# A four-layer graph network: fourth layer in another order of groups, with each tile's end between the groups

## The chip, the cores and the metric

The kernel runs on one core of a Trainium2 chip. The metric is the device time of one execution in microseconds (us).

## What is computed

`x` holds 4096 nodes of 128 features, `adj` is a sparse 4096 x 4096 matrix whose first nodes have far more neighbours than the last. Each of four layers adds to `x` a function of `h = relu(layernorm(x))` and `adj`. The fourth is an attention over neighbours with four heads of 32 features:

```python
q, k, v = (x @ W + b).reshape(n, H, C)           # for each of the three
attn = jnp.einsum('nhc,mhc->hnm', q, k) / np.float32(np.sqrt(C))
neg = jnp.where(mask[None], -jnp.inf, attn)      # mask = adj == 0
m = jnp.max(neg, axis=-1, keepdims=True)
e = jnp.where(mask[None], 0.0, jnp.exp(neg - m))
alpha = e / jnp.sum(e, axis=-1, keepdims=True)
out = jnp.einsum('hnm,mhc->hnc', alpha, v)       # then to (n, 128)
x_r = x @ Ws + bs
beta = sigmoid(concatenate([out, x_r, out - x_r], axis=-1) @ Wb)
return beta * x_r + (1.0 - beta) * out
```

## The kernel before, in words

The nodes are cut into 32 tiles of 128. While the first layer streams `adj`, lists of each tile's neighbours are made, cut into groups (called quads in the code) of up to 384 neighbours and the tile's own 128. The number of groups depends on the data: every tile has at least one, and some of the first have more. `bounds` holds each tile's first group, `quad_tile` each group's tile, and the groups stand in the order of the tiles.

The fourth layer works group by group. For a group, GpSimd (`gather_nodes(3)`, L797) gathers three blocks of 128 rows of keys and values from the table `kv_table` by indirect DMA. SyncE (`load_adj(3)`) loads the group's mask (L583), its tile's queries (L584) and the tile's own key and value rows (L600). TensorE turns the key rows (`turn_rows`, L1912), makes the four heads' scores (`scores`, L1922), turns the exponentials chunk by chunk (`turn_exps`, L1931), and multiplies them with the values (`values`, L1941). ScalarE takes the exponentials (`exps3`, L1029) and copies keys and even chunks out of the matrix engine's memory. VectorE subtracts the mask and takes the maximum (`scores`, L1575), keeps the running maximum of a tile (`maxima3`, L1583 to L1585; the table `cap` resets it where a new tile begins), copies the odd chunks (`turned3`, L1591) and adds the group's result to its tile's row of `acc3`, scaled by the change of the maximum (`add_up3`, L1603 to L1608).

These are a software pipeline: in step g VectorE copies chunk 3 of g, makes the maxima of g + 2, copies chunk 1 of g + 1 and adds up g (`step3`). SyncE and GpSimd load for g + 3. Each engine has its own queue and waits on semaphores. A step's instructions are written out for 7 turns of 4 steps (`PLAIN = 7`), and the rest is a loop of `further` turns of 4, which is 3 here: 40 steps. In written-out steps the gathers take their indices from `node_flat`; in looped ones from `stage`, into which SyncE loads three columns per group first.

Behind the last step comes `finish3` on VectorE: for each of four tile groups (`FT = 8` tiles, 1024 columns) it divides by the sums (L1627, after one reciprocal L1656), multiplies with gate weights (L1631), sums them (L1634, L1635), subtracts the skip term (L1636), makes the gate of the tile group before (L1640, L1641), and adds to `x_sb` (L1646, `blend`; L1652, `blend_tiles` for the last, eight instructions). ScalarE takes exponentials of the gates and multiplies the tiles by their gates (L1065, L1070, `scale`). SyncE then stores the 512 KB of each tile group (L690).

The second layer runs over the same groups. The third layer multiplies the denser part of `adj` as a dense product on TensorE (`dense`, L1877) and the rest group by group; VectorE copies indices (L1486) and adds each group (L1489) there.

## Time and profile before

| | |
|---|---|
| median of 3 runs | 1197.55 us (1195.87 to 1203.04) |
| the profiled execution | 1189.68 us, of which the span is 1188.0 us |
| TensorE busy | 895.1 us (75%) |
| VectorE busy | 822.4 us (69%) |
| ScalarE busy | 687.1 us (58%) |
| GpSimd busy | 509.9 us (43%) |
| mean granted TensorE clock | 0.85 of 2.4 GHz |

The profile shows one execution. Busy is the time in which an engine works on an instruction; waits and register work are not in it. The span goes from the first to the last instruction. In the rows below DVE is VectorE, ACT ScalarE, PE TensorE (PEld its weight loads), POOL GpSimd, SPq the queue of SyncE. A row of the order of time gives start and length in us, engine, line, operation, what is written and read, and in brackets the idle time of the engine before it and what ended it.

### The profile page before, as it was taken

The numbers are of one execution on the slowest core, as the hardware profiler recorded it, in microseconds if no ns is written. First come the engines' busy times: TensorE is split into PE (matmuls) and PEld (weight loads), VectorE is DVE, ScalarE is ACT, GpSimd is POOL, SyncE is SP. The second block draws the span as 40 slices with busy tenths as digits, with TensorE's granted clock in tenths as the row PEclk, the third lists the DMA queues.
The fourth block names the chain that finished last, engine by engine and source line by source line (L and its number), as shares of the span: only waits on it lengthen the run. The fifth ranks groups of instructions, "written<-read, shape, count | busy, mean of one in ns | idle before, by whom it ended". The sixth has DMA issues, their size and how long they took to land.

```text
span 1188.0 us, 25534 instructions
## 1 busy us (share of the span) xinstructions
PE 895.1 (75%) x5768; PEld 569.3 (48%) x5768; DVE 822.4 (69%) x2230; ACT 687.1 (58%) x3070; POOL 509.9 (43%) x526
## 2 busy tenths in 40 slices
PE   4979999999999352666667469997667788888750
PEld 1535555556455221555556334554444555555540
DVE  7388879879788774666665761121655888888788
ACT  4999879987977031434433351000455778888762
POOL 4002767735333434555555401666214444444420
PEclk9999988988989575676665679998897999999985
DMA  9556657657450125444444538984233444444421
GB/s 367 192 207 244 241 205 290 231 203 262 170 188 27 54 86 169 133 134 134 127 121 119 179 109 343 356 290 116 89 126 111 121 116 119 120 123 122 119 72 71
DMA packets 109354, 196.19 MB, mean 165 GB/s; under 512 B 21152, under 2 KB 93088, under 8 KB 103488
## 3 DMA queue, kind: packets, MB, share of 16 engines
q1 hardware_dynamic: 84368, 74.10, 19.8%
q10 hardware_dynamic: 8448, 82.99, 18.0%
q0 software_dynamic: 16432, 37.97, 11.7%
q8 instruction: 31, 0.51, 0.2%
q14 instruction: 75, 0.61, 0.2%
HBM read 166.17 MB, written 25.97 MB: 162 GB/s over the span
## 4 chain that ended last, share of the span: by engine, by line
PE 42%; DVE 22%; issue 17%; ACT 7%; another core or an unknown queue 2%; DVEq 2%; SPq 1%; DMA 1%; POOL 1%; ACTq 0%; POOLq 0%
PE ps L1877 7%; PE ps L1768 7%; PE ps L1852 4%; ACT unread L936 4%; PE ps L1931 4%; DVE work L1265 4%; PE ps L1922 3%; DVE work L1575 3%; PE ps L1794 2%; PE ps L1836 2%; DVE work L1266 2%; PE ps L1720 2%; PE ps L1716 2%; PE ps L1845 1%
## 5 line engine op out<-in xcount | busy, mean ns | idle before, releaser
L936 ACT ACTIVATE unread<-work 128x128 bf16<-128x128 f32 x1024 | 300.7, 295 | 6.9 <-ACT unread L936 2.1
L1768 PE MATMUL ps<-work,h_wide 128*128 128x512 f32 x512 | 241.8, 629 | 17.3 <-ACT h_wide L848 17.3
L936 ACT ACTIVATION_READ_ACCUMULATOR unread<-work 128x1 f32 x1024 | 191.6, 187 | 0.0
L755 POOL DMA_INDIRECT work<-in_adj_rows,adj_stage x120 | 157.3, 1311 | 60.1 <-issue 32.9
L1768 PEld LDWEIGHTS ps<-work,h_wide 128*128 128x128 f32 x512 | 101.3, 203 | 140.3 <-issue 138.6
L797 POOL DMA_INDIRECT work<-h_table,stage x105 | 100.2, 954 | 126.7 <-DMA h_table<-h_wide 59.3
L797 POOL DMA_INDIRECT work<-kv_table,node_flat x93 | 89.1, 958 | 121.7 <-PE ps L1941 77.5
L1575 DVE CUSTOM_DVE_ANT_0 work<-ps,work 128x512 f32<-128x512 f32 x168 | 116.2, 747 | 22.0 <-PE ps L1922 20.0
L1931 PE MATMUL ps<-ident,work 128*128 128x128 f32 x648 | 95.9, 281 | 42.6 <-issue 22.6
L1029 ACT ACTIVATE work<-work 128x512 f32<-128x512 f32 x165 | 117.2, 713 | 11.9 <-DVE work L1584 7.8
L797 POOL DMA_INDIRECT work<-h_table,node_flat x93 | 88.5, 951 | 71.8 <-issue 38.6
L1852 PE MATMUL ps<-work 128*128 128x128 f32 x320 | 72.0, 395 | 50.5 <-ACT work L977 30.8
L746 POOL COPY adj_stage<-adj_flat 128x3 int32 x40 | 24.1, 601 | 188.4 <-issue 178.6
L1931 PEld LDWEIGHTS ps<-ident,work 128*128 128x128 f32 x648 | 70.5, 141 | 62.8 <-issue 32.3
L1852 PEld LDWEIGHTS ps<-work 128*128 128x128 f32 x320 | 61.4, 286 | 64.8 <-ACT work L977 40.1
L977 ACT ACTIVATE work<-ps 128x512 f32<-128x512 f32 x40 | 23.9, 598 | 117.6 <-PE ps L1845 56.7
L1747 PE MATMUL ps<-work 128*32 128x128 f16 x1024 | 68.3, 422 | 29.9 <-DVE work L1192 20.0
L1877 PE MATMUL ps<-work,h_wide 128*128 128x512 f32 x192 | 85.3, 593 | 1.4 <-issue 0.8
L1836 PE MATMUL ps<-ident,work 128*128 128x128 f32 x164 | 40.7, 397 | 43.4 <-issue 35.4
L1189 DVE TENSOR_TENSOR work<-iota_s,slot 128x4096 f16<-128x4096 f16 x32 | 73.1, 2286 | 0.0
L1265 DVE TENSOR_TENSOR work<-work 128x2048 f32<-128x2048 f32 x32 | 73.1, 2283 | 0.1
L1591 DVE COPY work<-ps 128x512 f32<-128x512 f32 x81 | 55.7, 687 | 12.2 <-issue 6.3
(230 smaller groups left out, 1655.7 us busy)
## 6 DMA issues: line engine op xcount, KB each, us to landing
work<-in_adj_rows ACTq DMA_DIRECT2D x38, 2048.0 KB
work<-adj_table SPq DMA_DIRECT2D x66, 192.0 KB
work<-in_adj_rows SPq DMA_DIRECT2D x6, 2048.0 KB
mask_table<-work SPq DMA_DIRECT2D x43, 128.0 KB
work<-mask_table SPq DMA_DIRECT2D x43, 128.0 KB
work<-kv_table SPq DMA_DIRECT2D x43, 128.0 KB
adj_table<-work SPq DMA_DIRECT2D x42, 128.0 KB
work<-in_adj_rows SPq DMA_DIRECT2D x66, 64.0 KB
```

Source lines behind the costliest of these rows:

```text
L755: nc.gpsimd.indirect_dma_start(out=ag[:, h, c, :], out_offset=None, in_=adj_rows, in_offset=bass.IndirectOffsetOnAxis(ap=adj_stage[:, h // ...
L797: nc.gpsimd.indirect_dma_start(out=rows[:, b, c, :], out_offset=None, in_=table, in_offset=bass.IndirectOffsetOnAxis(ap=at, axis=0)).then_ ...
L936: ins = nc.scalar.activation(unread[:, m % (MQ // 2) * TB + t, :], ring[:, q, m, t * P:(t + 1) * P], ACT.Abs, accum_out=seen[:, b, t, q * ...
L1029: nc.scalar.activation(e[:, g.u % 2, h, :], e[:, g.u % 2, h, :], ACT.Exp, bias=nbest3[:, b, h:h + 1], scale=SCALE, accum_out=part3[:, b, h ...
L1189: nc.vector.tensor_tensor(onehot[:, b, :, :], iota_s[:, :, :], slot[:, j:j + 1, :] .to_broadcast([P, P, T]), ALU.is_equal)
L1265: link(nc.vector.tensor_tensor(half_sum, ring[:, q, 0:MQ // 2, :], ring[:, q, MQ // 2:MQ, :], ALU.add))
L1575: nc.vector.tensor_tensor_reduce(out=e[:, g.u % 2, h, :], in0=ps[:, 1 + h, :], in1=mk[:, b, :], scale=1.0, scalar=capped3[:, b, h:h + 1], ...
L1747: ins = mm(ps[NC * g:NC * g + NC, 7 if j % 2 else 3, 0:P], coded[:, j % 2, 0, :, m], onehot[:, j % 2, :, m], start=(m < 4), stop=(m >= T - 4))
L1768: ins = mm(ps[:, 0, :], h_sb[:, q * MQ + m, :], ring[:, q, m, :], start=(q + m == 0), stop=False)
L1852: ins = mm(ps[:, 4 + g.u % 2, 0:P], eT[:, c, 0, :], hg1[:, b, c, 0:P], start=(c == 0), stop=(c == QC - 1))
L1877: ins = mm(ps[:, 4 + nb, :], h_sb[:, m, :], ring2[:, q, m % MQ, :], start=(m == 0), stop=(m == T - 1))
L1931: ins = nc.tensor.transpose(ps[:, 5 + c % 2, h * P:(h + 1) * P], e[:, g.u % 2, h, c * P:(c + 1) * P], ident[:, :])
```

## The change

The order of groups in the fourth layer changes. First come the further groups, those of a tile beyond one, then each tile's last group in the order of the tiles. VectorE, ScalarE and SyncE run one looped turn (`looped_turns3`: the 10 turns less 9, at least one) and then 36 steps written out (`each_late`, class `Late`): 4 more for further groups, then 32, of which step k has the tile k - 4 as a constant. TensorE and GpSimd keep 7 written-out turns and 3 looped ones.

A tile's running maximum no longer stands in the group before it. A table `best_tab` with a column set per tile keeps it; in looped steps VectorE writes it and reads that of the next group's tile with a wait between.

Which groups are the further ones is worked out by VectorE in the third layer: two tables (`extra_tile`, `extra_unit`) from six comparisons and sums of 128 x 1792 elements, three before its steps there and three between the first. GpSimd makes one more row of numbers.

SyncE reads a group's number from a table and loads its three index columns into `stage` in every step of the fourth layer, and every gather of GpSimd waits for SyncE's three loads.

The end is cut into parts of 8 tiles. Behind a written-out step with tile t of 8 or more, VectorE does part t modulo 8 for tile group t // 8 - 1: 0 reciprocal and outputs, 1 products, 2 sums, 3 less skip, 4 gate, 7 blend; ScalarE takes the gate's exponential at 3 and multiplies four tiles at 5 and four at 6. `fin` has two buffers instead of four. SyncE stores the first two tile groups from inside its steps. Only the last tile group is left behind the steps.

```diff
+        class Late(Quad):
+
+            def __init__(self, turns, k):
+                super().__init__(turns + k // TURN if k // TURN else turns, k % TURN)
+                self.turns, self.k = turns, k
+                self.tile = min(k - TURN, T) if k >= TURN else None
+
+            def ahead(self, n):
+                return Late(self.turns, self.k + n)
+
+        def looped_turns3(eng):
+
+            return eng.value_load(stepsi[0:1, 2:3], min_val=1, max_val=STEPS - PLAIN)
+
+        def each_late(eng, body):
+
+            turns = looped_turns3(eng)
+            with eng.Fori(0, turns) as i:
+                for u in range(TURN):
+                    body(Quad(i, u))
+            for k in range(TURN + T):
+                body(Late(turns, k))
+            return turns + T // TURN + 1
 
...
                 def load(g):
                     q, b = g.q + begin, g.b
                     if k == 3:
-                        t = quad_value(sp, quad_tile, q, T)
-                        sp.dma_start(mk[:, b, :], mask_table[bass.ds(q * P, P), :]).then_inc(ac_full[k][b], 16)
+                        if g.tile is None:
+                            unit = quad_value(sp, extra_unit, g.q, QUADS)
+                            t = quad_value(sp, extra_tile, g.q, T)
+                        else:
+                            settle(sp)
+                            unit = sp.value_load(bounds[0:1, g.tile:g.tile + 1], min_val=0, max_val=QUADS)
+                            t = g.tile
+                        sp.dma_start(stage[:, b, :], node_flat[:, bass.ds(GC * unit, GC)]).then_inc(ac_full[k][b], 16)
+                        sp.dma_start(mk[:, b, :], mask_table[bass.ds(unit * P, P), :]).then_inc(ac_full[k][b], 16)
                         sp.dma_start(qs[:, b, :], qT[:, bass.ds(t * P, P)]).then_inc(ac_full[k][b], 16)
-                        return
+                        return T if g.tile is None else g.tile
...
+                        store_group(g.tile // FT - 2)
                 for b in range(bufs - 1):
...
+                steps = (sparse_quads(sp, step) if k == 2 else each_quad(sp, step) if k == 1 else
+                         each_late(sp, step))
...
+            def scale(i, half):
                 act.wait_ge(gate_ready, i + 1)
-                for j in range(FT):
-                    ins = nc.scalar.activation(fin[:, i, j, :], fin[:, i, j, :], ACT.Copy,
+                for j in range(FT // 2 * half, FT // 2 * half + FT // 2):
+                    ins = nc.scalar.activation(fin[:, i % 2, j, :], fin[:, i % 2, j, :], ACT.Copy,
                                                scale=zed3[:, FT * i + j:FT * i + j + 1])
                 ins.then_inc(scaled, 1)
 
-            for i in range(GROUPS):
-                exps_of(i)
-                if i < GROUPS - 1:
-                    scale(i)
+            def step_end3(g):
+                step3(g)
+                if g.tile is None or g.tile < FT:
+                    return
+                i, n = g.tile // FT - 1, g.tile % FT
+                if n == 3:
+                    exps_of(i)
+                elif n in (5, 6):
+                    scale(i, n - 5)
+
+            each_late(act, step_end3)
+            exps_of(GROUPS - 1)
 
...
+            def extra_tiles(n):
+                some = slice(NX // WAYS * n, NX // WAYS * n + NX // WAYS)
+                shape = [P, NX // WAYS, T]
+                is_past = work[:, 21504:21504 + NX // WAYS * T].rearrange("p (e t) -> p e t", t=T)
+                extra_link(nc.vector.tensor_tensor(is_past, extra_ends[:, :].rearrange("p (a t) -> p a t", a=1).to_broadcast(shape),
+                                                   iota_x[:, some].rearrange("p (e a) -> p e a", a=1).to_broadcast(shape), ALU.is_le))
+                extra_link(nc.vector.tensor_reduce(cap[:, some], is_past, AX.X, ALU.add))
...
+
+            dve.wait_ge(iotas, 20)
+            extra_link(nc.vector.tensor_tensor(extra_ends[:, :], ends[:, 1:T + 1], iota_x[:, 1:T + 1], ALU.subtract))
+            for n in range(WAYS // 2):
+                extra_tiles(n)
...
             def dense_added(j):
+                if j < 2 * (WAYS // 2) and j % 2:
+                    extra_tiles(WAYS // 2 + j // 2)
+                if j == 2 * (WAYS // 2):
+                    extra_units()
...
                 nc.vector.tensor_scalar(nbest3[:, b, :], best3[:, b, :], -SCALE, None, ALU.mult).then_inc(mx_ready[3], 1)
-                nc.vector.tensor_scalar(capped3[:, (b + 1) % NBUF, :], best3[:, b, :], cap[:, bass.ds(q + 1, 1)], None,
-                                        ALU.min).then_inc(cap_ready, 1)
+                after = capped3[:, (b + 1) % NBUF, :]
+                if g.tile is not None:
+                    nc.vector.tensor_copy(after, best_of(g.ahead(1).tile)).then_inc(cap_ready, 2)
+                    return
+                t, t_after = tile_at(g), tile_at(g.ahead(1))
+                nc.vector.tensor_copy(best_of(t), best3[:, b, :]).then_inc(cap_ready, 1)
+                dve.wait_ge(cap_ready, 2 * q + 3)
+                settle(dve)
+                nc.vector.tensor_copy(after, best_of(t_after)).then_inc(cap_ready, 1)
...
+            def outputs3(i):
+                tiles, outs, zeds = group3(i)
+                end_link(nc.vector.reciprocal(rden3[:, tiles, :].rearrange("p t (h a) -> p t h a", a=1), acc3[:, tiles, :, C:C + 1]))
+                end_link(nc.vector.tensor_tensor(outs.rearrange("p t (c h) -> p t h c", h=H), acc3[:, tiles, :, 0:C],
                                                  rden3[:, tiles, :].rearrange("p t (h a) -> p t h a", a=1)
                                                  .to_broadcast([P, FT, H, C]), ALU.mult))
...
+            def products3(i):
+                tiles, outs, zeds = group3(i)
+                end_link(nc.vector.tensor_tensor(prodw, outs, wide_row(wb_bc[:, 0:P]), ALU.mult))
+
+            def gate_sums3(i):
+                tiles, outs, zeds = group3(i)
+                sums = zeds.rearrange("p (t a) -> p t a", a=1)
+                end_link(nc.vector.tensor_reduce(zeds, prodw, AX.X, ALU.add))
+                nc.vector.tensor_tensor(sums, sums, xz[:, tiles, :], ALU.add).then_inc(z_ready, 1)
...
+            def blend3(i):
+                tiles, outs, zeds = group3(i)
+                dve.wait_ge(scaled, 2 * i + 2)
+                nc.vector.tensor_tensor(x_sb[:, tiles, :], outs, x_sb[:, tiles, :], ALU.add).then_inc(fin_ready, 1)
...
+            def step_end3(g):
+                step3(g)
+                if g.tile is None or g.tile < FT:
+                    return
+                part = {0: outputs3, 1: products3, 2: gate_sums3, 3: less_skip3, 4: gates3, 7: blend3}
+                if g.tile % FT in part:
+                    part[g.tile % FT](g.tile // FT - 1)
...
-            finish3()
+            each_late(dve, step_end3)
+            for part in (outputs3, products3, gate_sums3, less_skip3, gates3, blend_tiles3):
+                part(GROUPS - 1)
+            end_link.end()
...
             turn_exps(Quad(0, 0), (0, 1))
-            each_quad(pe, step3, further)
```

How rows move on VectorE. Before, this stands in a written-out step between a group's small maxima instructions and the next step (`link` and the names with `ready` or `done` are semaphores; `work` holds nearly all tiles):

```order
L1583 TENSOR_TENSOR work<-work 128x4 [waits s_read]
L1584 TENSOR_SCALAR work<-work 128x4
L1585 TENSOR_SCALAR work<-work,cap 128x4
L1591 COPY work<-ps 128x512 [waits pv_done3,eT_done3]
L472 TENSOR_LOAD quad_tile
L472 ISA x2
L1603 ISA [waits al_ready3,e_ready3]
L1603 TENSOR_TENSOR work<-work 128x132
L1605 ISA [waits link_u]
L1605 TENSOR_TENSOR work<-work 128x4
L1608 TENSOR_TENSOR work<-work,ps 128x4x32 [waits o_done]
L1591 COPY work<-ps 128x512 [waits pv_read3,pv_done3,eT_done3]
```

In the changed kernel this is the same place in the step with tile 8:

```order
L1670 TENSOR_TENSOR work<-work 128x4 [waits s_read]
L1671 TENSOR_SCALAR work<-work 128x4
L1674 COPY work<-best_tab 128x4
L1684 REGISTER_ALU [waits eT_done3]
L1685 COPY work<-ps 128x512 [waits pv_done3]
L1695 REGISTER_ALU [waits al_ready3]
L1697 TENSOR_TENSOR work<-work 128x132 [waits e_ready3]
L1699 TENSOR_TENSOR work<-work 128x4 [waits link_u]
L1702 TENSOR_TENSOR work<-work,ps 128x4x32 [waits o_done]
L1717 RECIPROCAL work<-work 128x32 [waits pv_read3]
L1718 TENSOR_TENSOR work<-work 128x8x4x32 [waits link_e3]
L1685 COPY work<-ps 128x512 [waits link_e3,pv_done3,eT_done3]
```

The table read (TENSOR_LOAD) is gone, a copy from `best_tab` stands for the operation with `cap`, and a reciprocal and the outputs of eight tiles (128x8x4x32) stand between the adding up and the next copy of chunk 3.

Behind the last step of VectorE, before, the first of four such turns and part of the next:

```order
L1656 RECIPROCAL work<-work 128x128 [waits e_ready3]
L1627 TENSOR_TENSOR work<-work 128x8x4x32 [waits link_e3]
L1631 TENSOR_TENSOR work<-work,wb_bc 128x1024 [waits link_e3]
L1634 TENSOR_REDUCE work<-work 128x8 [waits link_e3]
L1635 TENSOR_TENSOR work<-work,h_wide 128x8 [waits link_e3]
L1636 TENSOR_TENSOR work<-work,h_wide 128x1024
L1627 TENSOR_TENSOR work<-work 128x8x4x32
L1631 TENSOR_TENSOR work<-work,wb_bc 128x1024 [waits link_e3]
L1640 TENSOR_SCALAR work<-work 128x8 [waits link_e3,ez_ready]
L1641 RECIPROCAL work<-work 128x8 [waits link_e3]
L1634 TENSOR_REDUCE work<-work 128x8
L1635 TENSOR_TENSOR work<-work,h_wide 128x8 [waits link_e3]
```

and in the changed kernel all that is left there:

```order
L1717 RECIPROCAL work<-work 128x32
L1718 TENSOR_TENSOR work<-work 128x8x4x32 [waits link_e3]
L1724 TENSOR_TENSOR work<-work,wb_bc 128x1024 [waits link_e3]
L1729 TENSOR_REDUCE work<-work 128x8 [waits link_e3]
L1730 TENSOR_TENSOR work<-work,h_wide 128x8 [waits link_e3]
L1734 TENSOR_TENSOR work<-work,h_wide 128x1024
L1739 TENSOR_SCALAR work<-work 128x8 [waits ez_ready]
L1740 RECIPROCAL work<-work 128x8 [waits link_e3]
L1751 SCALAR_TENSOR_TENSOR x_sb<-work,x_sb 128x128 [waits gate_ready]
L1751 SCALAR_TENSOR_TENSOR x_sb<-work,x_sb 128x128 x7
```

Three of four tile groups have left this place.

On SyncE, a written-out step of the fourth layer before:

```order
L472 TENSOR_LOAD quad_tile [waits s_read]
L472 ISA x2
L583 DMA work<-mask_table 128x512
L584 ISA
L584 DMA work<-work 128x128
L472 TENSOR_LOAD quad_own [waits pv_done3]
L472 ISA x2
L600 ISA
L600 DMA work<-kv_table 128x256
```

and after, a step with a fixed tile:

```order
L600 ISA
L629 TENSOR_LOAD bounds [waits s_read]
L629 ISA x2
L631 ISA
L631 DMA stage<-node_flat 128x3
L632 ISA
L632 DMA work<-mask_table 128x512
L633 DMA work<-work 128x128
L677 REGISTER_ALU
L649 DMA work<-kv_table 128x256 [waits pv_done3]
```

An index load stands ahead of the mask's, the read of `quad_tile` became one of `bounds` ahead of all three loads, and the one of `quad_own` is gone.

## Rows read from the trace of the kernel before

**Rows 1.** Windows: length; busy us (instructions) of PE, PEld, DVE, ACT, POOL; PEclk, DMA share, GB/s

```profile
1010.80:1152.20 141.40, 113.79 (x1399) 77.77 (x1399) 118.29 (x371) 113.50 (x301) 63.38 (x67) 1.00 0.40 115
```

**Rows 2.** Order of time, VectorE, fourth layer, and the line of the adding up

```profile
1047.96 0.69 DVE L1591 COPY work<-ps 128x512 f32<-128x512 f32 x1 [0.17 <-issue]
...
1052.04 0.68 DVE L1591 COPY work<-ps 128x512 f32<-128x512 f32 x1
...
1053.85 0.69 DVE L1591 COPY work<-ps 128x512 f32<-128x512 f32 x1 [0.17 <-issue]
...
1055.21 0.75 DVE L1575 CUSTOM_DVE_ANT_0 work<-ps,work 128x512 f32<-128x512 f32 x1 [0.67 <-PE ps L1922]
...
1128.79 0.69 DVE L1591 COPY work<-ps 128x512 f32<-128x512 f32 x1 [0.68 <-issue]
...
L1603 DVE TENSOR_TENSOR work<-work x40: 295/296/355, 913.4 to 1151.4; 128x132 f32 x40
```

**Rows 3.** Order of time, ScalarE and TensorE, in the same group

```profile
1049.38 0.19 ACT L1029 ACTIVATION_READ_ACCUMULATOR work<-work 128x1 f32 x1
...
1049.61 1.09 PE L1931 MATMUL ps<-ident,work 128*128 128x128 f32 x8
```

**Rows 4.** Order of time, VectorE, behind the last group

```profile
1152.66 0.95 DVE L1656 RECIPROCAL work<-work 128x128 f32<-128x128 f32 x1 [0.42 <-DVE work L1608]
...
1155.78 1.23 DVE L1631 TENSOR_TENSOR work<-work,wb_bc 128x1024 f32<-128x1024 f32 x1
...
1159.65 1.95 DVE L1627 TENSOR_TENSOR work<-work 128x1024 f32<-128x1024 f32 x1
...
1167.18 1.96 DVE L1627 TENSOR_TENSOR work<-work 128x1024 f32<-128x1024 f32 x1
...
1182.74 2.19 DVE L1652 SCALAR_TENSOR_TENSOR x_sb<-work,x_sb 128x128 f32<-128x128 f32 x8
```

**Rows 5.** Lines of VectorE, 1010.8 to 1152: count, busy, mean ns, idle before

```profile
L1575 DVE CUSTOM_DVE_ANT_0 work<-ps,work 128x512 f32<-128x512 f32 x92 | 63.6, 747 | 4.2 <-PE ps L1922 3.4 <-issue 0.7
L1591 DVE COPY work<-ps 128x512 f32<-128x512 f32 x46 | 31.6, 687 | 7.4 <-issue 3.9 <-remote 1.4 <-DVE work L1608 1.2
```

**Rows 6.** Lines of ScalarE behind 1152

```profile
L1070 ACT ACTIVATE work<-work 128x128 f32<-128x128 f32 x24 | 7.3, 388 | 14.7 <-DVE work L1641 14.7
```

**Rows 7.** Order of time, start of the fourth layer, SyncE and GpSimd

```profile
883.70 0.35 SPq L583 DMA_DIRECT2D work<-mask_table  x1
...
885.00 0.95 POOL L797 DMA_INDIRECT work<-kv_table,node_flat  x1 [23.76 <-DMA kv_table<-work]
...
885.39 0.35 SPq L583 DMA_DIRECT2D work<-mask_table  x1
...
888.96 0.36 SPq L600 DMA_DIRECT2D work<-kv_table  x1
```

**Rows 8.** Order of time, GpSimd, a written-out group and a looped one

```profile
1044.60 0.94 POOL L797 DMA_INDIRECT work<-kv_table,node_flat  x1 [2.61 <-PE ps L1941]
...
1137.21 0.94 POOL L797 DMA_INDIRECT work<-kv_table,stage  x1 [2.74 <-DMA work<-work]
```

**Rows 9.** Order of time, VectorE, start of the third layer

```profile
744.94 0.17 DVE L1486 COPY stage<-node_flat 128x3 int32 x1 [24.40 <-DMA work<-h_table,stage]
...
758.37 0.29 DVE L1489 TENSOR_TENSOR work<-work,ps 128x128 f32 x1 [6.69 <-PE ps L1868]
```

**Rows 10.** Order of time, VectorE and GpSimd in the first layer

```profile
198.47 2.28 DVE L1265 TENSOR_TENSOR work<-work 128x2048 f32<-128x2048 f32 x1
...
199.38 2.21 POOL L755 DMA_INDIRECT work<-in_adj_rows,adj_stage  x1 [0.80 <-POOL adj_stage L746]
```

**Rows 11.** Windows (columns as in rows 1), where the fourth layer fills up

```profile
903.50:906.90 3.40, 1.50 (x8) 1.12 (x8) 2.37 (x10) 2.15 (x6) 0.00 (x0) 0.88 0.00 0
906.90:910.30 3.40, 3.40 (x43) 1.51 (x41) 1.59 (x4) 1.89 (x7) 0.00 (x0) 0.62 0.01 2
```

155 lines of the change are left out of this document (77 added, 78 removed).

## The prediction

> **What bounds the kernel now.** I read the stretches first. The fourth layer's groups run from 905 to 1152 us: each of the four computing engines is four fifths busy there and none is idle for long, so the question is who waits for whom. In the last 24 groups VectorE is busy 118.29 of 141.40 us, TensorE 113.79, ScalarE 113.50, at full TensorE clock [rows 1].
>
> The order of time on VectorE shows one group: a copy of chunk 3 at 1047.96, the four score maxima, a copy of chunk 1 at 1052.04, the adding up, and the next chunk 3 copy at 1053.85, 5.89 us after the first. The holes are 0.2 us long, and one of 0.67 us waits for TensorE's scores. TensorE waits in turn: its transposes at 1052.77 had waited 0.73 us for VectorE's copy [rows 3]. So VectorE binds, with TensorE's answer to it close behind. The 40 adding-up instructions start from 913.4 to 1151.4, so a group takes 6.10 us on average, against the 5.89 of the one looked at [rows 2].
>
> After the last group VectorE alone works from 1152.66 to its last instruction at 1182.74 + 2.19 = 1184.93, and the span ends with the last store at 1188.0 [rows 4]: 35.3 us that nothing else fills.
>
> **The change, term by term** (minus is faster), against the profiled execution's own 1189.68 us.
>
> 1. *The tail gives up three of its four tile groups.* What stays: a reciprocal of 32 columns instead of 128, from the row of 0.95 us [rows 4] no more than that and no less than a quarter of it, with its link about 0.4; then the fourth group. The group's turn lasts 1159.65 to 1167.18 = 7.53 us, of which the blend of the group before, about 1.15, goes away; the eight small blends add 2.19 and the store 3.07 [rows 4]. Together 0.4 + 6.4 + 2.2 + 3.1 = 12.1, so **12.1 - 35.3 = -23.2.**
>
> 2. *The same work comes back inside the loop.* Per group of 8 tiles six parts on VectorE: 7.53 us as in the tail, plus its own reciprocal 0.4. 3 x 7.9 = **+23.8**, if VectorE were without a hole. Terms 1 and 2 cancel: work moved along the engine that binds gains only what that engine wasted before.
>
> 3. *What it wasted.* In those 24 groups VectorE's idle time ahead of the maxima is 4.2 us and ahead of the copies 7.4 us [rows 5]. A part runs while TensorE computes the next scores, so the first kind vanishes behind a part; of the second kind, some 0.2 us behind every adding up is the link's own and stays. 18 of the 24 groups carry a part. Lower end: 18/24 of 4.2 = 3.2. Upper end: all 11.6. I take **-6**, near 24 times 6.10 less 5.89, which is 5.0, and nearer the middle since a part also covers the 0.2-us waits of such a group.
>
> 4. *ScalarE's scaling*, hidden behind VectorE before: 24 instructions, 7.3 us in all [rows 6], now four behind the group steps 5 and 6 of each eight. ScalarE's last exponential ended at 1049.57 and TensorE's transposes began at 1049.61 [rows 3], so lateness passes on at once; but VectorE picks up the result at 1052.04, 1.3 us after TensorE is done (1049.61 + 1.09). Two times 1.2 us late, less 1.3: 0.7 to 1.1 per eight tiles. Ends 0 and 7.9; **+2**.
>
> 5. *The start.* SyncE's loads per group lie 1.69 us apart (883.70, 885.39); each gets one more table read and one more DMA, the index load. I add 1.1 us for each, so that the own rows, issued at 888.96, go out about 3 us later, less the table reads that they lose. The first gather, at 885.00 [rows 7], now also waits until the index, mask and query loads have landed; the first maxima hang on both. Ends 0 and 4; **+3**.
>
> 6. *The gathers.* GpSimd's gathers waited for TensorE only in the 28 written-out groups; now all 40 wait for SyncE's loads too, as in the looped ones, where that DMA ended the wait [rows 8]. The looped groups took no longer for it, so +0; for the 8 groups that read two tables **+1** (ends 0 and 3).
>
> 7. *The rest.* Three stores of 512 KB now run beside the gathers: **+0.5** (0 to 3). VectorE turns back its loop once instead of three times; its hole at a turn was 0.68 us (1128.79) against 0.17 inside [rows 2], two turns fewer make **-1** (0 to -1).
>
> 8. *Third layer.* Six comparisons and six sums over 1792 columns for the table of tiles. From 1.23 us for 1024 columns [rows 4], 2.1 each, 26 us in all. Half of it stands where VectorE waits 24.40 us for the first gather, the other half in steps in which it waits up to 6.69 us for TensorE [rows 9], whose dense product runs on. Cost 0; without that cover it would be up to 26 us.
>
> Sum: -23.2 + 23.8 - 6 + 2 + 3 + 1 + 0.5 - 1 = +0.1, so 1189.8 us in a profiled execution. The three runs of before have a median of 1197.55, 7.87 above the profiled 1189.68; with the same distance 1197.7, in round numbers **1198 us**.
>
> On the gathers, a row and a rule beside each other. While VectorE's addition of two on-chip operands ran, 198.47 to 200.75, an indirect gather begun at 199.38 took 2.21 us; the gathers of the fourth layer's loop take 0.94 [rows 8, 10]. So 1.27 us per gather hit, and the parts with two such operands (outputs, products, less skip, blend) are of that kind; in the loop they follow the adding up, when the third gather has already begun. The Trainium skill (SBUF — State Buffer, "Who interferes with whom") says that a VectorE instruction with two SBUF inputs contends with a GpSimd instruction that reads SBUF, the one first issued blocking the other; the trace agrees. By that rule the gathers that start inside a part would be held, which is the second rival below.
>
> **The rivals.**
>
> *The holes take it all.* If VectorE's parts fall into every hole (11.6 instead of 6), scaling costs nothing and the start only 1: +0.1 - 5.6 - 2 - 2 = -9.5, 1188 us; with the looped groups' holes too, 1185. For it: even the group of 5.89 us holds waits of 0.2 us. Against it: most of these are links.
>
> *The gather chain becomes late* (slower). Place: GpSimd's wait for the index, mask and query loads, then TensorE's transposes of the rows. The price is up to 1.27 us in each of the 12 groups with a part of two operands, 15 us, less the 5 that longer groups give back: 1208. It decides from about 1.3 us of lateness in a group, which is what TensorE is ahead of VectorE's copy (term 4). For it: the looped groups' gathers start on a DMA's landing. Against: parts lengthen the group, so the chain gets more time.
>
> *TensorE's clock falls.* Between 903.5 and 906.9 the engine was busy for 1.50 us and stood for the rest, and the clock went from 2.4 to 1.2 GHz; a granted 0.88 there and 0.62 in the 3.4 us behind it mean 0.12 + 0.38 = 0.50 times 3.4, or 1.7 us of full clock lost [rows 11]. In the steady loop TensorE's hole ahead of VectorE's copy is 0.73 us in the group shown and the clock stays at 1.00 [rows 1, 3]. Now the outputs' part (the reciprocal and 1.95 us with its link) holds up the chunk 3 copy, hence TensorE's values, for 2.4 us [rows 4], a hole three times as long. A fall costs up to 1.7 us. Three falls: +5, 1203; at every one of the 18 parts: +31, 1229. For it: the hole's length. Against: work before and behind it is dense, and TensorE has 1.3 us to spare.
>
> **How the numbers follow.** A measurement of this kernel can tell about 1% (12 us) from no change. Forecast (1198, own range 1192 to 1204): 0.52. Holes take it all: 0.18, half of it beyond -12 with the median's own scatter (1195.87 to 1203.04). Gather chain: 0.12, half beyond +12. Clock: 0.18, two fifths beyond +12. Faster by over 1%: 0.10; slower: 0.06 + 0.07 + 0.01 = 0.14; within 1%: 0.76. The range leaves out the far part of the clock rival and of the holes: 1187 to 1212.
>
> **What would show it.** Term 1: VectorE's first instruction behind the last adding up lies 12 to 13 us before the end. Terms 2 and 3: the last 24 groups take 6.10 + (23.8 - 6)/24 = 6.84 us on average; 6.6 or less speaks for the first rival, over 7.2 for one of the other two. Term 4: ScalarE's waits shrink in steps 5 to 7. Term 5: TensorE's first transposes of layer four come 3 us later after the last row store. Term 6: transposes of rows that wait for a DMA, in many groups, would confirm the gather rival. Clock: a granted clock below 1.00 between 1010 and the last group. Term 8: the stretch of dense products, 720 to 820 us, is as long as before; if it grew, the sum's zero is wrong. The forecast as a whole fails if VectorE turns out not to bind: then the parts are free and the whole 23.2 us is gained.

## The result and the profile of the changed kernel

In 20 executions each the changed kernel takes 1205.99 us in the median (1199.54 to 1212.88), the kernel before 1195.67 (1183.97 to 1204.34). The ratio of the changed kernel to the kernel before is 1.0116, with a 95% interval of 1.0094 to 1.0137: slower by 1.2 per cent, between 11 and 16 us. The two medians as they stand lie 10.3 us apart, 0.9 per cent, since the ratio and its interval are estimated from the executions within 1.5 per cent of each kernel's fastest. The forecast was 1198 with a range of 1187 to 1212; the time is inside the range and 8 us above the forecast.

The profiled execution took 1206.02 us with a span of 1204.3, where the kernel before had 1188.0. The page's line of busy times, and its rows of TensorE's busy time and granted clock over 40 slices of 30 us:

```profile
PE 892.6 (74%) x5768; PEld 565.8 (47%) x5768; DVE 848.3 (70%) x2258; ACT 686.5 (57%) x3070; POOL 522.2 (43%) x527
...
PE   4979999999998244556566379997766678777674
...
PEclk9988999988998675776766579999786999999997
```

TensorE's row ended in 50 before, one slice and a half in which VectorE worked alone, and ends in 74 now. But the whole is longer, so time was lost elsewhere.

Windows of the fourth layer (columns as in rows 1): its fill with the first steps, the steps up to the 17th adding up, the last 24, and the tail.

```profile
905.00:960.00 55.00, 36.97 (x345) 24.04 (x345) 32.88 (x104) 29.78 (x78) 19.86 (x21) 0.79 0.33 95
960.00:1034.80 74.80, 59.68 (x735) 41.49 (x732) 61.77 (x197) 59.98 (x158) 35.03 (x37) 1.00 0.43 119
1034.80:1190.20 155.40, 114.10 (x1399) 77.33 (x1399) 135.87 (x396) 118.90 (x325) 64.51 (x68) 0.99 0.40 113
1190.20:1204.30 14.10, 0.28 (x2) 0.00 (x0) 10.31 (x21) 1.51 (x4) 0.00 (x0) 0.62 0.18 74
```

The third of these answers [rows 1]: 155.40 us with VectorE busy for 135.87, where 141.40 us had 118.29. The granted clock was 0.99 over it, and a finer row of windows shows 1.00 in every 6.5 us up to 1184.5. In the last 5.7 us of it, 1184.5 to 1190.2, it was 0.74 (0.97 from 1146.5 to 1152.2 in the kernel before), and the last group took 7.80 us instead of 6.89 in the changed kernel's second profile. The first window's 0.79 is the fill.

The last step of the adding up (before: line 1608, 914.0 to 1152.0; that of [rows 2] stands 0.6 us ahead of it), by line:

```profile
L1702 DVE TENSOR_TENSOR work<-work,ps x40: 275/289/290, 931.1 to 1190.6; 128x128 f32<-128x128 f32 x32, 128x128 f32 x8
```

Forty of them now take 259.5 us from first to last, 238.0 before. The last 24 lie 6.76 us apart on average, the first sixteen intervals sum to 104.1 us and not 97.5; the first four are 8.22, 7.86, 7.56 and 8.70 us, later ones without a part 5.7.

Such a slow group in order of time on VectorE, one of the looped further groups (what stands behind "idle before" is in brackets):

```profile
927.37 0.16 DVE L1671 TENSOR_SCALAR work<-work 128x4 f32<-128x4 f32 x1
928.89 0.17 DVE L1677 COPY best_tab<-work 128x4 f32 x1 [1.36 <-issue]
929.26 0.38 DVE L1680 COPY work<-best_tab 128x4 f32 x1 [0.20 <-DVE best_tab L1677]
929.45 0.69 DVE L1685 COPY work<-ps 128x512 f32<-128x512 f32 x1
```

And the same two copies by line, 914 to 960 us (count, busy and mean, idle before):

```profile
L1677 DVE COPY best_tab<-work 128x4 f32 x6 | 1.2, 208 | 7.7 <-issue 7.7
L1680 DVE COPY work<-best_tab 128x4 f32 x6 | 1.2, 206 | 1.2 <-DVE best_tab L1677 1.2
```

Between the scaled maximum (927.37) and the copy into the tile's table (928.89) VectorE stands for 1.36 us with nothing to wait for ("issue"): it reads two tile numbers into registers. Six such pairs of copies cost 7.7 us of standing and 1.2 more for the second copy's wait on the first. My sum had 1 us for it, in term 6.

VectorE by line in the last 24 groups, against [rows 5], and one of the parts:

```profile
L1662 DVE CUSTOM_DVE_ANT_0 work<-ps,work 128x512 f32<-128x512 f32 x92 | 63.5, 747 | 1.9 <-PE ps L2019 1.3 <-issue 0.5
...
L1685 DVE COPY work<-ps 128x512 f32<-128x512 f32 x47 | 32.3, 687 | 8.4 <-PE ps L2028 6.1 <-issue 1.2 <-DVE work L1718 0.5
...
L1718 DVE TENSOR_TENSOR work<-work 128x1024 f32<-128x1024 f32 x3 | 6.2, 2059 | 0.3
```

The idle time ahead of the maxima fell from 4.2 to 1.9 us, that ahead of the chunk copies rose from 7.4 to 8.4.

The tail behind the last adding up, against [rows 4]:

```profile
1191.04 1.23 DVE L1745 TENSOR_TENSOR x_sb<-work,x_sb 128x1024 f32<-128x1024 f32 x1
...
1199.09 2.19 DVE L1751 SCALAR_TENSOR_TENSOR x_sb<-work,x_sb 128x128 f32<-128x128 f32 x8
```

From 1191.04 to 1204.3 are 13.3 us, 35.3 before. The first instruction there (L1745, 1.23 us) is the blend of the third tile group: tile 31 is the last step, so this one part of the eighteen stands behind the loop and not in it. The start, against [rows 7]:

```profile
895.87 0.54 SPq L631 DMA_DIRECT2D stage<-node_flat  x1
...
897.19 0.53 SPq L633 DMA_DIRECT2D work<-work  x1
...
899.00 0.50 SPq L631 DMA_DIRECT2D stage<-node_flat  x1
...
899.85 0.95 POOL L844 DMA_INDIRECT work<-kv_table,stage  x1 [27.07 <-DMA work<-work]
...
904.03 1.46 SPq L649 DMA_DIRECT2D work<-kv_table  x3
```

The loads of a group lie 3.13 us apart (895.87, 899.00) where they lay 1.69. GpSimd's first gather, which stood 4.1 us behind the last projection (885.00 less 880.9), stands 7.5 us behind it (899.85 less 892.4).

And in the third layer, VectorE's table instructions beside GpSimd's gathers:

```profile
765.66 2.02 DVE L1568 TENSOR_TENSOR work<-extra_ends,work 128x1792 f32<-128x1792 f32 x1
...
765.88 2.63 POOL L844 DMA_INDIRECT work<-h_table,stage  x1 [3.59 <-PE ps L1965]
...
774.60 2.02 DVE L1568 TENSOR_TENSOR work<-extra_ends,work 128x1792 f32<-128x1792 f32 x1
...
774.71 2.74 POOL L844 DMA_INDIRECT work<-h_table,stage  x1 [0.30 <-issue]
```

Two gathers that begin just behind such an instruction's start take 2.63 and 2.74 us instead of 0.95.

### The profile page after: what moved, and what is told of

It reads as the page before. It is cut to its first block, busy times and chain, and to the rows that moved or that the text cites. A ratio compares the mean times of both kernels' runs of the same rounds, so it can differ in the third digit from the quotient of the medians.

```text
span 1204.3 us, 25750 instructions
## 1 busy us (share of the span) xinstructions
PE 892.6 (74%) x5768; PEld 565.8 (47%) x5768; DVE 848.3 (70%) x2258; ACT 686.5 (57%) x3070; POOL 522.2 (43%) x527
## 3 DMA queue, kind: packets, MB, share of 16 engines
q0 software_dynamic: 16432, 37.97, 11.6%
## 4 chain that ended last, share of the span: by engine, by line
PE 36%; DVE 26%; issue 19%; ACT 4%; another core or an unknown queue 4%; SPq 3%; DVEq 3%; DMA 1%; POOL 0%; ACTq 0%; POOLq 0%
PE ps L1865 7%; DVE work L1321 4%; DVE work L1662 4%; PE ps L2028 3%; PE ps L1974 3%; PE ps L1949 3%; PE ps L1891 2%; PE ps L2019 2%; DVE work L1322 2%; PE ps L1813 2%; PE ps L1817 2%; PE ps L1933 1%; PE ps L1844 1%; PE ps L2038 1%
## 5 line engine op out<-in xcount | busy, mean ns | idle before, releaser
L844 POOL DMA_INDIRECT work<-kv_table,stage x129 | 123.2, 955 | 187.6 <-PE ps L2038 105.4
L802 POOL DMA_INDIRECT work<-in_adj_rows,adj_stage x120 | 162.2, 1352 | 58.9 <-issue 34.7
L844 POOL DMA_INDIRECT work<-h_table,stage x105 | 104.5, 995 | 130.5 <-DMA h_table<-h_wide 57.2
L1685 DVE COPY work<-ps 128x512 f32<-128x512 f32 x81 | 55.7, 688 | 12.7 <-PE ps L2028 6.9
```

Source lines behind the costliest of these rows:

```text
L802: nc.gpsimd.indirect_dma_start(out=ag[:, h, c, :], out_offset=None, in_=adj_rows, in_offset=bass.IndirectOffsetOnAxis(ap=adj_stage[:, h // ...
L844: nc.gpsimd.indirect_dma_start(out=rows[:, b, c, :], out_offset=None, in_=table, in_offset=bass.IndirectOffsetOnAxis(ap=at, axis=0)).then_ ...
```

## Where the time went, by stages

Each row is one profiled execution; the marks are starts of named lines. "Third": from the layer's first dense matmul to the last projection matmul behind it. "Fill": from there to the first adding up. Then 16 intervals between adding ups, the last 23, and from the last adding up to the end of the span. The kernels further down are those of the experiments; the four of the last block ran on a third chip, on which every kernel is 5 to 6 per cent faster (see the end).

| kernel | third | fill | 16 steps | last 23 | tail |
|---|---|---|---|---|---|
| before | 161.5 | 33.1 | 97.5 | 140.5 | 36.0 |
| before_again | 163.1 | 31.8 | 96.9 | 143.8 | 36.1 |
| tables_before | 170.1 | 33.1 | 97.1 | 142.1 | 36.1 |
| changed | 166.3 | 38.7 | 104.1 | 155.4 | 13.7 |
| after_again | 171.7 | 40.3 | 106.5 | 155.5 | 13.7 |
| tables_ahead | 170.0 | 38.3 | 107.5 | 156.3 | 13.7 |
| end_behind | 166.3 | 39.6 | 104.9 | 138.9 | 36.5 |
| no_read_in_maxima | 168.8 | 34.7 | 103.9 | 153.5 | 13.7 |
| lists_first | 171.6 | 38.6 | 104.2 | 154.6 | 13.7 |
| both | 168.1 | 33.3 | 101.5 | 153.9 | 13.7 |
| small_tables | 155.5 | 34.0 | 99.1 | 152.4 | 13.6 |
| reads_ahead | 155.3 | 33.5 | 99.1 | 152.6 | 13.6 |
| reads_ahead_end_behind | 155.5 | 34.0 | 99.4 | 132.1 | 36.5 |
| read_in_each | 152.1 | 39.7 | 102.9 | 155.7 | 13.7 |

From the first profile to that of the changed kernel: third +4.8, fill +5.6, 16 steps +6.6, last 23 +14.9, tail -22.3, and 6.7 us ahead of the third layer, where both kernels run the same code. Together 16.3, the difference of the spans. The second profile of before (before_again) shows the 6.7 to be chance: its first dense matmul stands at 726.4 us, the changed kernel's at 726.1, the first profile's at 719.4. Taking the means of the two profiles of each, the layers in question give +6.7, +7.0, +8.1, +13.3 and -22.4: 12.7 us, inside the 11 to 16 that the ratio gives.

The 16 steps hold two opposite things. The first five grew from 30.6 to 39.2 us, the other eleven fell from 66.9 to 65.0.

## The experiments

The first four ran on one chip (kernel before: 1206.8 us there), the next four on another (1192.1), the last four on a third (1132.2). The chip of the first comparison is not on record. Ratios are to the kernel before on the same chip. Single executions of one kernel on the first chip lay up to 27 us apart, so the stages of the profiles carry more there than the times.

### The end put back behind the loop

```
-            each_late(dve, step_end3)
-            for part in (outputs3, products3, gate_sums3, less_skip3, gates3, blend_tiles3):
-                part(GROUPS - 1)
+            each_late(dve, step3)
+            for i in range(GROUPS):
+                outputs3(i)
+                products3(i)
+                if i:
+                    gates3(i - 1)
+                gate_sums3(i)
+                less_skip3(i)
+                if i:
+                    blend3(i - 1)
+            gates3(GROUPS - 1)
+            blend_tiles3(GROUPS - 1)
```

ScalarE's exponentials and scalings and SyncE's stores follow the loop likewise.

> The changed kernel with its new order of groups, but with the end of all 32 tiles put behind the loop again, on VectorE, ScalarE and SyncE. Theory A (VectorE is full in the late groups, so that the parts cost in the loop what they cost behind it): a late group falls from 6.76 us back to 5.7 to 5.9, that is 20 to 24 us less over the last 24 groups, and the tail behind the last adding up grows from 14.2 to 36.7 us, 22.5 more: the time stays within 3 us of the changed kernel, 1204 to 1209 us. Theory B (the parts lie in waits of VectorE's, which was the idea behind the rival of 1188 us): the late groups become only some 8 us shorter, the tail 22.5 longer, and the kernel takes about 1220 us.

Measured: ratio 1.0124 (1.0063 to 1.0185), with the changed kernel not beside it. The last 23 intervals between adding ups and the tail (columns as in rows 1):

```profile
1045.60:1184.50 138.90, 112.91 (x1399) 78.29 (x1396) 114.92 (x369) 113.20 (x299) 63.43 (x67) 1.00 0.42 117
1184.50:1221.00 36.50, 0.00 (x0) 0.00 (x0) 31.18 (x45) 7.84 (x28) 0.00 (x0) 0.51 0.15 58
```

The late groups take 6.04 us each with no part in them, the changed kernel's 6.76: 16.5 us over 23 intervals for 22.8 us of tail. So the move by itself gains some 6 us by the stages, between my two theories. The 16.5 compares two chips; the other two kernels of this chip that keep the parts in the loop take 153.5 and 156.3 us for the 23 intervals, 14.6 and 17.4 more than here. VectorE is busy for 114.92 of these 138.90 us; in the changed kernel for 135.87 of 155.40. Its idle time is 24.0 us without the parts and 19.5 with them: of 21.0 us more work 4.5 went into waits. That is term 3, sized 6 in the prediction.

### The tables of the third layer, in the kernel before

```
+            dve.wait_ge(iotas, 20)
+            extra_link(nc.vector.tensor_tensor(extra_ends[:, :], ends[:, 1:T + 1], iota_x[:, 1:T + 1], ALU.subtract))
+            for n in range(WAYS // 2):
+                extra_tiles(n)
...
             def dense_added(j):
+                if j < 2 * (WAYS // 2) and j % 2:
+                    extra_tiles(WAYS // 2 + j // 2)
+                if j == 2 * (WAYS // 2):
+                    extra_units()
```

The results go to a buffer that nothing reads.

> The kernel before, with only the changed kernel's extra tables added to its third layer (three pairs of instructions ahead of the loop, three in it, and the unit numbers), nothing of which is read. Theory A (the tables in the third layer's loop hold GpSimd's gathers and so TensorE, which is where the third layer's 8 us more come from): the third layer takes 119 instead of 111 us and the kernel 4 to 8 us more than before, 1200 to 1204 us. Theory B (my prediction's term of 0: the tables lie beside the dense blocks, and the two profiles differ for another reason): within 2 us of the kernel before, 1195 to 1198 us.

Measured: ratio 0.999 (0.9938 to 1.0043), but a third layer of 170.1 us against 161.5 and 163.1. In order of time, this kernel's first dense matmul being at 730.1:

```profile
769.28 0.29 DVE L1497 TENSOR_TENSOR work<-work,ps 128x128 f32 x1 [6.77 <-PE ps L1902]
...
769.67 2.02 DVE L1521 TENSOR_TENSOR work<-extra_ends,work 128x1792 f32<-128x1792 f32 x1
...
769.89 2.63 POOL L804 DMA_INDIRECT work<-h_table,stage  x1 [3.74 <-PE ps L1902]
...
776.73 0.29 DVE L1497 TENSOR_TENSOR work<-work,ps 128x128 f32 x1
```

And the second profile of the kernel before, its first dense matmul at 726.4:

```profile
765.51 0.29 DVE L1489 TENSOR_TENSOR work<-work,ps 128x128 f32 x1 [7.49 <-remote]
...
765.97 0.69 DVE L1510 TENSOR_TENSOR work<-work,ps 128x512 f32<-128x512 f32 x1 [0.17 <-DVE work L1489]
...
766.12 0.94 POOL L797 DMA_INDIRECT work<-h_table,stage  x1 [3.63 <-PE ps L1868]
...
768.72 0.29 DVE L1489 TENSOR_TENSOR work<-work,ps 128x128 f32 x1
```

The addition of the third sparse group follows the first dense matmul after 42.3 us in before_again (768.72) and after 46.6 here (776.73). The gather that follows TensorE takes 2.63 instead of 0.94 us, the block's addition waits behind the table pair, and the next group behind both. In all seven profiles of the first two chips and the changed kernel's own that have three pairs in the loop, that addition stands at 46.4 to 46.9 us, in the two of before at 42.2 and 42.3. The lateness is thus shown. Its price is not. Up to the layer's last gathered matmul this kernel takes 114.8 us, before 111.2 and 111.9: the tables alone cost 3 us there, and not the 8 of theory A. Over the whole layer the profiles with the tables lie 3 to 10 us above those without, and the time, whose interval ends at +5 us, confirms none of it. My estimate for the third layer's cost is some 5 us.

### The tables ahead of the third layer's loop

```
             for n in range(WAYS // 2):
                 extra_tiles(n)
```

becomes `for n in range(WAYS)`, with the unit numbers behind it and nothing in the loop.

> The changed kernel with all six pairs of the extra tables and the unit numbers ahead of the third layer's loop, where VectorE idles 11 us behind the first three pairs; none in the loop. Theory A (the pairs in the loop cost the gathers their place): 4 to 8 us less than the changed kernel, 1198 to 1202 us, and no gather above 2 us between 760 and 790 us. Theory B (no cost there): within 2 us of the changed kernel. Third case: the three more pairs, 12 us of VectorE ahead of the loop, make the first adding up late; then the third layer is longer still.

Measured: ratio 1.0044 (1.0005 to 1.0082), against the 1.0116 and 1.0137 of the changed kernel in other comparisons. Its profiled execution, 1220.07 us, is one of the longest of its twelve (1199.85 to 1224.03), so I read the places of its rows and not the length of its layers. Rows at the end of the six pairs:

```profile
752.08 2.02 DVE L1568 TENSOR_TENSOR work<-extra_ends,work 128x1792 f32<-128x1792 f32 x1
...
752.55 2.38 POOL L844 DMA_INDIRECT work<-h_table,stage  x1 [0.30 <-issue]
...
763.26 0.29 DVE L1545 TENSOR_TENSOR work<-work,ps 128x128 f32 x1
```

With six pairs the last ones run into the first gathers, which take 2.38 and 2.69 us. VectorE's first addition comes 30.7 us behind the first dense matmul; in the other profiles of the first two chips and the changed kernel's own it comes at 28.8 to 31.4, so the third case is not shown. The third addition stands at 45.8, 3.5 us late instead of 4.4. The gathers are held at either place. The time, if anything, is 0.7 to 0.9 per cent lower than with three pairs in the loop, across chips; that was not compared on one chip and stays open.

### No table read in the maxima

```
-                t, t_after = tile_at(g), tile_at(g.ahead(1))
-                nc.vector.tensor_copy(best_of(t), best3[:, b, :]).then_inc(cap_ready, 1)
-                dve.wait_ge(cap_ready, 2 * q + 3)
-                settle(dve)
-                nc.vector.tensor_copy(after, best_of(t_after)).then_inc(cap_ready, 1)
+                nc.vector.tensor_scalar(after, best3[:, b, :], fresh[:, bass.ds(q + 1, 1)], None,
+                                        ALU.min).then_inc(cap_ready, 2)
...
             def step3(g):
                 turned3(g, 3)
+                t = tile_at(g)
+                if not isinstance(g, Late) or g.k < 2:
+                    nc.vector.tensor_copy(best_of(t), best3[:, g.b, :])
```

The last two further groups keep the old way, since tile 0's last group reads the table right behind them.

> The changed kernel with one thing else in its further groups: the maximum is capped by a table of flags (as in the kernel before), so that no tile number is read between the maximum and its hand-over; the tile's maximum is written to its table at the start of the group's own step. Only two of eight further groups keep the old way. Theory A (the two reads of a tile number in front of the copies are what makes the first five steps 8.2 instead of 6.1 us): the first five steps take 6.0 to 6.6 us each, some 7 us less in all, and the kernel 1198 to 1201 us. Theory B (the fill of the layer is slow because the gathers and their lists come late, whatever VectorE does): the first steps stay near 8 us and the time within 2 us of the changed kernel.

Measured: ratio 0.9898 (0.9855 to 0.9941). The first five steps take 6.39, 6.31, 6.15, 8.63 and 7.63 us; they were 8.22, 7.86, 7.56, 8.70 and 6.84. The three mended ones are 4.8 us shorter, and the fill, which holds three such maxima, 4 (34.7 for 38.7). The other thirteen steps are some 4.5 us longer than in the changed kernel's profile, 2.4 of it one wait of VectorE for "remote" in the seventh (8.07 us), so that the 16 steps as a whole are as long as there. Fill and 16 steps together take 138.6 us, those of end_behind on the same chip 144.5, those of the changed kernel's first profile 142.8. The same place as above, from the kernel "both", which has this mending:

```profile
921.98 0.16 DVE L1686 TENSOR_SCALAR work<-work 128x4 f32<-128x4 f32 x1
922.09 0.23 DVE L1697 TENSOR_SCALAR work<-work,quad_first 128x4 f32<-128x4 f32 x1
922.29 0.69 DVE L1703 COPY work<-ps 128x512 f32<-128x512 f32 x1
```

No standing is left between the scaled maximum and the cap. So the reads cost 4 to 6 us by the stages. The time says more: by the ratios 1.5 per cent less than tables_ahead beside it, 17 us, and by the medians of all twelve executions 14 (1198.3 and 1212.6). No stage shows the rest, and with executions up to 27 us apart I don't read it as an effect. By the ratio this kernel is also 1 per cent faster than the kernel before; the stages don't show that either (see "A version that beats both?").

### The changed kernel again, and the lists of the first groups loaded early

> The changed kernel itself, beside the next three on one chip. On the chip of the first four experiments the kernel before took 1206.8 us and not 1195.7, and single executions lay 20 us apart, so these need the changed kernel measured beside them. If the tile numbers read in the maxima cost what their stage in the profile shows (7 to 8 us), it stands some 1.1 per cent above the kernel before. If it stands 2 per cent above it here, the reads cost more than any stage of the profiles shows.

Measured: 1210.55 us, ratio 1.0137 (1.0086 to 1.0188), which agrees with the 1.0116 of the first comparison.

The second kernel:

```
+            for b in range(NBUF - 1):
+                unit = quad_value(sp, extra_unit, b, QUADS)
+                sp.dma_start(stage[:, b, :], node_flat[:, bass.ds(GC * unit, GC)]).then_inc(stage_first, 16)
             store_rows(3)
...
+                    elif k == 3 and isinstance(g.q, int) and g.q < NBUF - 1:
+                        pool.wait_ge(stage_first, 16 * (NBUF - 1))
```

> The changed kernel with the node lists of the fourth layer's first three groups loaded ahead of the third layer's last stores, so that GpSimd's first gather waits for the last stored row only, as in the kernel before, and not for three loads of its group. Theory A (the extra load is on the path that fills the layer): GpSimd's first gather 3 to 4 us earlier against the last projection (6.4 us behind VectorE's last instruction of it in the changed kernel, 3.1 us before), and 3 us less in all. Theory B (the own rows, which follow nine loads of SyncE 3.1 us apart, are what is late): the first gather is earlier, the first transpose is not, and the time within 1 us of the changed kernel.

Measured: ratio 1.0111 (1.0061 to 1.0162). In order of time, the last projection matmul being at 894.6:

```profile
898.80 2.00 POOL L856 DMA_INDIRECT work<-kv_table,stage  x1 [23.77 <-DMA kv_table<-work]
...
904.13 1.41 SPq L651 DMA_DIRECT2D work<-kv_table  x3
...
908.41 1.09 PE L2021 MATMUL ps<-ident,work 128*128 128x128 f32 x4 [13.09 <-DMA work<-kv_table]
```

The first gather starts 4.2 us behind the last projection, as before, and not 7.5. But the own rows go out 9.5 us behind it (11.6 in the changed kernel, 8.1 before), the first transposes follow 13.8 us behind it (15.3; 10.7), and the first adding up comes after 38.6 us. That is as in the changed kernel's first profile (38.7) and 1.7 us less than in after_again on this chip (40.3). Neither theory came as stated: the first gather gained 3.3 us, the first transposes 1.5, the fill between nothing and 1.7. The first gather itself took 2.00 us and not 0.95 here.

### Both mendings

> The changed kernel with both mendings: no tile number read in the maxima of the looped further groups, and the first three node lists loaded early. If the two costs lie behind one another, the sum of both: 7 + 3 us less than the changed kernel, 2 us more than the kernel before at most and perhaps 2 us less. If one hides the other (the fill waits for whichever is last), only the larger of the two, 7 us.

Measured: 1200.09 us, ratio 1.0062 (1.0039 to 1.0086), that is 9 us less than the changed kernel beside it (1.0137). Fill and 16 steps take 134.8 us; 146.8 in after_again, 142.8 in lists_first, and 130.6 and 128.7 in the profiles of before. With the reads gone the early lists are worth 1.4 us of fill (33.3 against no_read_in_maxima's 34.7, on another chip). What is left against before are the two steps that keep the old way, 8.44 and 8.43 us where before has 6.34 and 6.20; the second of them holds a wait of 1.13 us for TensorE.

### The kernel before, profiled again

> The kernel before, profiled once more, for how far its stages differ from one execution to the next. If the second layer takes 207 to 209 us here (201.4 in the first profile, 209.4 in the changed kernel's, whose second layer is the same code), its 8 us are chance; the same for the third layer's 111.2 against 119.5. If both come out as in the first profile, the changed kernel has a cost there that is not named yet.

Measured: 1199.76 us. The second layer, from its first to its last aggregating matmul, takes 207.7 us; 201.4 in the first profile, 209.4 in the changed kernel: chance. From the first dense matmul to the last gathered one, the third layer takes 111.9 us, 111.2 in the first profile and 119.5 in the changed kernel: not chance.

### Small tables

```
-                extra_link(nc.vector.tensor_tensor(is_past, extra_ends[:, :].rearrange("p (a t) -> p a t", a=1).to_broadcast(shape),
-                                                   iota_x[:, some].rearrange("p (e a) -> p e a", a=1).to_broadcast(shape), ALU.is_le))
-                extra_link(nc.vector.tensor_reduce(cap[:, some], is_past, AX.X, ALU.add))
+                extra_link(nc.vector.tensor_tensor(qcmp[:, :, :], extra_ends[:, :].rearrange("p (a t) -> p a t", a=1).to_broadcast(shape),
+                                                   qnum[:, :].rearrange("p (c a) -> p c a", a=1).to_broadcast(shape), ALU.is_le))
+                extra_link(nc.vector.tensor_reduce(qval[:, 0, :], qcmp[:, :, :], AX.X, ALU.add))
+                for c in range(3):
+                    ins = nc.vector.tensor_scalar(qdiag[:, c, :], ident[:, :], qval[:, 0, c:c + 1], None, ALU.mult)
+                ins.then_inc(qv_ready, 1)
...
+            pe.wait_ge(qv_ready, 3)
+            mm(ps[:, 1, P:4 * P], ones[:, :], qdiag[:, :, :].rearrange("p c n -> p (c n)"), start=True,
+               stop=True).then_inc(qv_done, 1)
```

> The kernel of the label both, but the further groups' tile numbers are made as those of all groups are: each partition compares its own three group numbers with the 32 tile ends (128x96 instead of six times 128x1792), and TensorE turns them into a row with one 384 column matmul behind the third layer's first dense blocks. 24 us of VectorE's become about 1. Theory A (the long two-input table instructions hold GpSimd's gathers and VectorE's adding in the third layer: 42.2 becomes 46.6 us behind the layer's first dense matmul in all five kernels that have three pairs in the loop, and 42.2 or 42.3 in both profiles of before): the third addition falls back to 42.3 us behind the first dense matmul, the layer takes 112 to 114 us and not 118 to 120, and the kernel 5 to 8 us less than both, at or below the kernel before. Theory B (the third layer's length hangs on how the dense blocks arrive, which the earlier order of SyncE changes): it stays at 118 us and the time at that of both.

Measured: 1138.64 us, ratio 1.006 (1.0033 to 1.0087). The third layer with its projection takes 155.5 us here; but read_in_each, which has the long tables and ran on the same chip, takes 152.1, and from the first dense matmul to the first projection both take 108.5 and 108.3. On this chip the third sparse group's addition stands at 40.6 us with the small tables and 41.0 with the long ones. The next ones are up to 1.2 us late with the long tables, and from the ninth on there is no difference. So the question was not answered: on this chip the long tables cost nothing that could be taken away.

### The last tile numbers read at the start of the step

```
                 if not isinstance(g, Late) or g.k < 2:
                     nc.vector.tensor_copy(best_of(t), best3[:, g.b, :])
+                    if isinstance(g, Late):
+                        two = tile_at(g.ahead(2)), tile_at(g.ahead(3))
                 scores(g.ahead(2))
-                maxima3(g.ahead(2))
+                maxima3(g.ahead(2), *two)
```

> As small_tables, and in the last two further groups the tile numbers are read at the start of the step and no longer between the maximum and its copies. Those two steps took 8.4 us each in the kernel both, the others 6.2. If the place of the reads is what counts, they take 6.2 to 6.6 us, 4 us less in all; if it is their number, they stay at 8.4. With all three mendings the fourth layer behind its last projection should take 298 us instead of before's 307 or 308, and the kernel be 0.5 to 0.8 per cent faster than the kernel before.

Measured: 1141.99 us, ratio 1.010 (1.0065 to 1.0135). The two steps take 8.43 and 7.28 us, in small_tables 8.42 and 7.26. A miss. VectorE in small_tables:

```profile
892.51 0.23 DVE L1686 TENSOR_SCALAR work<-work 128x4 f32<-128x4 f32 x1
893.30 0.17 DVE L1692 COPY best_tab<-work 128x4 f32 x1 [0.57 <-issue]
894.38 0.17 DVE L1695 COPY work<-best_tab 128x4 f32 x1 [0.91 <-DVE best_tab L1692]
```

and in reads_ahead:

```profile
888.89 0.75 DVE L1677 CUSTOM_DVE_ANT_0 work<-ps,work 128x512 f32<-128x512 f32 x1 [1.85 <-PE ps L2054]
...
891.85 0.16 DVE L1686 TENSOR_SCALAR work<-work 128x4 f32<-128x4 f32 x1
...
891.94 0.17 DVE L1692 COPY best_tab<-work 128x4 f32 x1
...
892.31 0.17 DVE L1695 COPY work<-best_tab 128x4 f32 x1 [0.19 <-DVE best_tab L1692]
```

The standing ahead of the two copies went from 0.57 and 0.91 us to nothing and 0.19. In its place VectorE now stands 1.85 us ahead of the first maximum at 888.89, where it stood 0.48 in small_tables. The profile puts that wait down to TensorE's transposes, but VectorE's own queue shows the reads in it. Line 508 is the helper that reads a table value into a register; its loads and the last piece of each read between 886.8 and 888.8 us (count, ns, first and last start):

```profile
L508 DVEq TENSOR_LOAD <-qdiag x2: 300/302/304, 886.9 to 887.7; - x2
L508 DVEq SEQ_ASSERT  x2: 23/23/23, 887.5 to 888.2; - x2
```

The second read starts 0.7 us behind the first and ends at 888.2, the maximum's own register work follows, and it starts at 888.89. So the reads were moved and not hidden: 1.3 us went at the copies, 1.4 came ahead of the maximum. The expectation's other branch came true, the number of reads counts. The step with two of them takes 8.43 us at the old place and 8.42 at the new one, the step with one 7.25 and 7.29, and the step behind them with none 6.38 and 6.40. A read takes some 0.7 us of VectorE's queue, and what it costs is what the instruction ahead of it leaves uncovered: at the copies only operations of 0.16 to 0.23 us stand ahead.

### The same with the end behind the loop

The edit is that of the first experiment, made to reads_ahead.

> As reads_ahead, with the end of all tiles behind the loop again. What the move of the end is worth by itself, now that the start no longer blurs it. By the profiles of the first experiment (last 24 steps 6.04 us without parts, 6.76 with, 17 us; tail 36.5 against 13.7, 23 us) the move is worth 6 us, so this takes 6 us more than reads_ahead. By my prediction's sum the parts cost 23.8 less 6 in the loop and the tail gives 23.2: 5 us more. If VectorE were full already, it would take the same time.

Measured: 1142.79 us, ratio 1.0089 (1.005 to 1.0128), the same as reads_ahead's 1.010. The last 24 groups of reads_ahead, then of this kernel:

```profile
965.20:1117.80 152.60, 115.62 (x1398) 79.68 (x1395) 136.22 (x395) 118.47 (x324) 63.03 (x67) 0.97 0.40 114
```

```profile
970.40:1102.50 132.10, 110.80 (x1399) 76.95 (x1397) 115.09 (x369) 110.36 (x301) 63.14 (x67) 1.00 0.44 124
```

Here the late groups without parts take 5.74 us and VectorE is busy for 115.09 of 132.10; with the parts 136.22 of 152.60. 21.1 us more work made the stretch 20.5 us longer. On this chip next to nothing went into waits: VectorE's idle time is 16.4 us with the parts and 17.0 without, and the move gains 2.4 us by the stages (20.5 against 22.9) and nothing that the times show.

### One read more in each late group

```
                 t = tile_at(g)
+                if g.tile is not None:
+                    quad_value(dve, quad_tile, g.q, T)
```

> The changed kernel with one tile number more read in each of the 32 last groups, at the head of the adding up, where the kernel before reads it, and not used. What a read costs there: if the 5.7 us of the changed kernel's plain steps against 5.88 before come from the constant tile numbers, the plain steps go back to 5.9, and the last 24 by 0 to 0.2 us each; if the read lies in a wait, nothing changes.

Measured once: 1154.65 us. The steps 9 to 16, which have the read and no part, take 5.78 us on average (5.77 in small_tables). The steps with a part, where VectorE has no hole, go from 7.89, 6.62, 6.62, 6.32 to 8.14, 6.92, 6.93, 6.65: 0.25 to 0.33 us for one read where VectorE is full, and nothing where it waits anyway. That is less than the 0.7 us of a read above, because this one runs under a copy of 0.69 us: in the trace both begin at 990.41 and the read ends at 991.07.

## The prediction, step by step

**Term 1, the tail** (-23.2): right in kind, -22.3. VectorE's first instruction behind the last adding up stands 13.3 us before the end, where 12 to 13 were named and 12.1 summed. The difference is the third tile group's blend of 1.23 us, which the term took out of the tail and term 2 put into the loop; it stands behind the last step.

**Terms 2 and 3, the parts in the loop** (+23.8 - 6, that is 6.84 us a group): right in kind, 3 to 5 us too high, 1.2 of it the blend. Measured 6.76 and +14.9 us, on the means +13.3, without the third blend; against the same order without parts +16.5 us beside a profile of the first chip, with 4.5 us of the work gone into waits, and +20.5 on the third, with 0.6. The named sign of the first rival, 6.6 or less, did not come. Not priced was that a late group without parts is itself shorter than before, 6.04 against 6.11 and 6.25, which fits a tile number that is now a constant and no longer read.

**Term 4, ScalarE's scaling** (+2): not visible by itself. It is inside the 6.76.

**Term 5, the start** (+3, ends 0 and 4): its mechanism is there, but its total is too small. The fill grew by 5.6, on the means 7.0. The loads did lie 1.4 us further apart and the own rows went out 3.5 us later, as the term said; what it left out is that the first three maxima stand in the fill, each with its reads. Without the reads the fill was 4.0 us shorter, and the early lists then gave 1.4 more: the larger share is the reads and not the loads.

**Term 6, the further groups** (+1, ends 0 and 3): the step that failed. It said "for the 8 groups that read two tables +1" and counted only SyncE's and GpSimd's side. On VectorE a read takes some 0.7 us of its queue: 0.3 us where a long instruction stands ahead of it, 1.17 to 1.36 for a pair where only a short one does, and the pair stood between the maximum and its hand-over. The first five steps, which have such reads, grew by 8.5 us (39.2 for 30.6) and the 16 steps by 6.6, on the means 8.1. Shown by the edit without the reads are 4.8 us of the first three steps and 4.0 of the fill; the fourth and fifth step keep their length when the reads stand elsewhere in them, and shrink with the number of reads (8.4, 7.3, 6.4 us for two, one, none). That is more than 0.7 us a read; the copies and their wait on one another are in it too, and it is not split further. Fill and steps together were 4 to 6 us shorter without the first reads, and with the early lists too 8 to 12 (134.8 for 142.8 and 146.8). A hint was there: ahead of the first adding-up instruction, where the kernel before reads its tile number, VectorE stood 1.9 us in 6 places with nothing to wait for, and I took that for links.

**Term 7** (-1 for the loop turns, +0.5 for the stores): nothing in the profiles contradicts its turns, and nothing shows them either. It counted three stores beside the gathers; only two stand in the loop, since the third blend is behind it. The groups' plain steps fell to 5.7 in the changed kernel's own profile.

**Term 8, the third layer** (0, "without that cover up to 26"): wrong on two chips, by an estimated 5 us (3 up to the last gathered matmul with the tables alone), right on the third. Its 26 us of work were twelve instructions of 2.02, 24. The cover held VectorE's own time, but not GpSimd's: gathers that begin inside a two-operand table instruction took 1.93 to 2.74 us, each ending some 0.8 us behind that instruction. That is the rule of the Trainium skill (SBUF — State Buffer, "Who interferes with whom") which the prediction weighed for the end's parts only. The trace agrees with it at every one of these places in the changed kernel; I had not laid it beside term 8. A held gather does not always cost time: read_in_each on the third chip has gathers of 2.65 and 2.54 us there, and the first projection comes no later (108.3 us; 108.5 with the small tables). For the parts it mattered little: over the last 24 groups of the changed kernel one gather began inside a part of two operands. It took 1.65 us, the longest of the fourth layer (before: 1.96); the mean was 0.96 in both kernels.

**The rivals.** *Holes take it all*: fell. *Gather chain late*: fell, the late groups took 6.76 and not above 7.2. *TensorE's clock falls*: fell; the granted clock was 1.00 up to 1184.5 us, through all the parts, and TensorE's waits beside the outputs' part did not bring it down. The 0.74 of the last 5.7 us stands behind the parts. The slower result came by none of the rivals but by terms 5, 6 and 8, which I had summed to 4 and which made 17 to 22.

**Why inside the range nonetheless:** the large terms, 1 to 4, summed to -3.4 and measured -7.4 (-9.1 on the means: last 23 and tail), 4 to 6 us in the kernel's favour; the small ones erred by 13 to 18 us the other way. That the two sides cancelled so far is luck, and so are 2 us of the base: the forecast stood on a median of 1197.55 where twenty executions gave 1195.67. The change itself was forecast at +0.1 us and measured at 10 to 16, and slower by more than 1 per cent had been given a chance of 0.14; the ratio of 1.0116 is there.

## A version that beats both?

None that holds. One measurement says otherwise: no_read_in_maxima stands 1.0 per cent below the kernel before on the first chip (0.9898, interval 0.9855 to 0.9941). But its five stages sum to 474.6 us, those of the two profiles of before to 468.6 and 471.7, and "both", which adds the early lists to the same mending, ends above the kernel before on the second chip. It was not run a second time, and whether it is faster stays open.

"Both" takes away 9 us of the changed kernel's 16 on its chip (1.0137 to 1.0062) and ends 0.6 per cent above the kernel before; with the small tables it ends 0.6 per cent above it on the third chip as well. There was no profile of the kernel before on that chip, so where those 7 us stand is open. An estimate from the rows: the fourth layer of small_tables takes 299.1 us behind the last projection, and that of before, with 5.8 us for each of 39 steps, 33 of fill and 36 of tail, would take 295. Of the 4 us between them the first 16 steps cost 6 (99.1 for 92.8) and the fill 1, and the move of the end gives back 3 (22.4 of tail for 19.0 in the loop).

## What to carry to other kernels

Work moved along the engine that binds gains only that engine's waits: here 23 us of tail cost 15 to 21 us in the loop, so the first question is how long the engine stood before, not how long the tail is. Against a gain of a few microseconds the side costs decide, and the ones that stand in no list of busy times: a table value read into a register stops the engine's queue for some 0.7 us here, and only a long instruction just ahead of it covers that. So count the reads in the binding engine's queue and pass on values that need no address: moving a read elsewhere in the same step gained nothing. And price what hides "beside" other work twice, once for its own engine and once for the engine that it keeps from the memory.

## What the runs showed that was not expected

The three chips differ by 6 per cent with the same kernel (1206.8, 1192.1, 1132.2 us). Much of it stands in the second layer, where first and last aggregating matmul lie 201.4 to 213.3 us apart in the profiles of the first two and of the first comparison, and 164.5 to 171.3 on the third. ScalarE's copy there, 520 to 600 us, from "both":

```profile
L1039 ACT ACTIVATE work<-ps 128x512 f32<-128x512 f32 x16 | 9.6, 597 | 46.8 <-PE ps L1962 23.2 <-remote 18.7 <-issue 4.9
```

and from small_tables on the third chip:

```profile
L1039 ACT ACTIVATE work<-ps 128x512 f32<-128x512 f32 x19 | 11.3, 597 | 34.5 <-PE ps L1962 34.5
```

"Remote" are waits that end on nothing the profile can name: 18.7 us of ScalarE's idle time in 80 us on the one, none on the other. Those four are up to 5.7 us long; the 7.49 ahead of the addition in before_again is another. What they are I can't say.

On the faster chip the same change is worth something else: the late groups without parts took 5.74 us instead of 6.04, the parts filled next to none of VectorE's idle time (16.4 us with them, 17.0 without), and the move of the end gained 2 us instead of 6.
